# Expert choice for four images at a time, with new stage borders and a new order in one shared PSUM bank

## The reference

```python
for layer in (0, 1):
    sa, ca, ga, sb, cb, gb = (silu(c[layer]) @ wmod[layer]).reshape(32, 6, 1, 128)   # ga, gb: bounded below
    h = layernorm(x) * (1 + ca) + sa
    x = x + ga * attention(h)         # 16 heads of 8; layer 0 with a bias by distance, layer 1 with its own norm
    h = layernorm(x) * (1 + cb) + sb
    logits = h @ gate                 # 8 experts
    # layer 0: the best two experts of each token, with normalised weights; layer 1: the best one
    x = x + gb * sum(weight[e] * expert[e](h) for e in chosen(logits))   # 128 -> 512 -> 128
```

## Time and profile before

| | us |
|---|---|
| median of 3 runs | 2106.24 (2105.88 to 2109.68) |
| profiled execution | 2108.88 |
| its span, first to last instruction | 2107.1 |
| granted TensorE clock, mean | 0.923 |
| PE busy | 1613.4 (77%) |
| DVE busy | 1494.7 (71%) |
| ACT busy | 1137.7 (54%) |
| POOL busy | 667.5 (32%) |

### The profile page before, as it was taken

One profiled execution on the slowest core, in us unless ns is written; L12 is line 12 of the kernel. 1 busy time (PEld: TensorE's weight loads), 2 busy tenths in 40 slices (PEclk: granted clock), 3 DMA queues, 4 the chain that ended last, 5 costly groups with the idle time before them and its releaser, 6 DMA issues. The chain is left out here.

```text
span 2107.1 us, 43953 instructions
## 1 busy us (share of the span) xinstructions
PE 1613.4 (77%) x14050; PEld 1155.9 (55%) x14050; DVE 1494.7 (71%) x4845; ACT 1137.7 (54%) x2198; POOL 667.5 (32%) x740
## 2 busy tenths in 40 slices
PE   2488888888888845999963777877877877843996
PEld 1266565656566624999951444444544444523886
DVE  4478888888888734777744787788888788833664
ACT  0277777777677631222211676666666666641543
POOL 0011323232323252555531223233333333230544
PEclk9899999999999977999985898899999999976998
DMA  3333343333333313222235445455455545415443
GB/s 106 85 69 69 79 79 77 79 76 80 77 79 79 67 39 83 72 72 74 72 104 126 85 95 122 97 108 119 102 108 113 109 101 110 91 59 169 133 125 81
DMA packets 267612, 193.24 MB, mean 92 GB/s; under 512 B 26111, under 2 KB 257441, under 8 KB 266612
## 3 DMA queue, kind: packets, MB, share of 16 engines
q1 hardware_dynamic: 252024, 155.41, 35.2%
q0 software_dynamic: 15360, 35.03, 5.4%
HBM read 95.34 MB, written 53.18 MB: 70 GB/s over the span
## 5 line engine op out<-in xcount | busy, mean ns | idle before, releaser
L923 DVE TENSOR_REDUCE mx<-A 128x2 f32<-128x512 f32 x1024 | 688.4, 682 | 213.7 <-PE A L1173 197.3
L753 ACT ACTIVATE probs<-B 128x1024 f32<-128x1024 f32 x512 | 521.8, 1019 | 281.1 <-PE B L1200 154.6
L1173 PE MATMUL A<-stack 126*128 126x256 bf16 x2048 | 398.3, 284 | 113.4 <-DVE mx L923 92.3
L1200 PE MATMUL B<-stack 128*128 128x256 bf16 x2048 | 367.0, 282 | 67.4 <-DMA stack<-mrow 66.7
L1173 PEld LDWEIGHTS A<-stack 126*128 126x128 bf16 x2048 | 169.6, 100 | 266.8 <-DVE mx L923 165.4
L1218 PE MATMUL M<-probs,vals 128*32 128x256 f32 x4096 | 295.1, 408 | 23.8 <-DVE On L946 19.7
L1200 PEld LDWEIGHTS B<-stack 128*128 128x128 bf16 x2048 | 199.4, 102 | 122.3 <-DMA stack<-mrow 82.0
L640 POOL DMA_INDIRECT gathered<-h,slot_in x192 | 186.9, 974 | 128.6 <-DVE slot_in L1056 82.3
L1629 PE MATMUL A<-w2s,hid 128*128 128x128 f32 x1792 | 219.5, 276 | 8.5 <-issue 8.5
L604 POOL TENSOR_TENSOR parts<-rem,parts 128x512 bf16<-128x512 f32 x64 | 74.5, 1165 | 468.1 <-ACT parts L732 468.1
L1629 PEld LDWEIGHTS A<-w2s,hid 128*128 128x128 f32 x1792 | 208.8, 192 | 12.9 <-issue 11.8
(11 more groups left out here) (182 smaller groups left out, 2405.5 us busy)
## 6 DMA issues: line engine op xcount, KB each, us to landing
stack<-parts SPq DMA_DIRECT2D x768, 64.0 KB
xt<-gathered SPq DMA_DIRECT2D x112, 132.0 KB, 2.2
probs<-gathered SPq DMA_DIRECT2D x40, 256.0 KB
w<-in_w SPq DMA_DIRECT2D x4, 2048.0 KB, 10.1
back_rows<-mod_rows SPq DMA_DIRECT2D x64, 128.0 KB, 3.7
x_mid<-X SPq DMA_DIRECT2D x64, 128.0 KB, 2.9
hid<-expert_out SPq DMA_DIRECT2D x64, 128.0 KB
X<-in_x SPq DMA_DIRECT2D x32, 128.0 KB, 3.8
```

The lines of the kernel that those rows point to most:

```text
L753: act.activation(probs[c % 4][:, :, :, :], Bp[BUFFER[c]][:, :, :, :], ACT.Exp, scale=EXP_SCALE[l][c // 4]).then_inc(b_exp.handle, 1)
L923: dve.tensor_reduce(mx[u][:, h, :], A[h % 2][:, :, :], AX.X, ALU.max).then_inc(a_max.handle, 1)
L1173: ins = pe.matmul(A[h % 2][:, t, :], stack[u][0:n, h, 0, t * P:(t + 1) * P], stack[u][0:n, h, 1, :], start=True, stop=True)
L1200: ins = pe.matmul(Bp[BUFFER[c]][:, j, t, :], stack[u][:, h, 1, t * P:(t + 1) * P], stack[u][:, h, 0, :], start=True, stop=(l == 1))
```

## The change

- GROUP goes from 2 to 4, HELD from 4 to 8, LAG from 5 to 7; an image is scattered at i - 7. The sizes of routing operations double, their number halves. `h3` and the experts' tiles (`w1s`, `w2s`, `hid`) share one piece of SBUF, and `Y` lies in `yt`.
- Setup: the three loads of the modulation go first and have a semaphore of their own; both layers' products are made in separate banks and rows; POOL clears `stack`.
- The experts' weights are loaded in 16 (layer 1: 18) pieces, one at the end of a tick. The padding and the table of tiles are done at the end of attention.
- In layer 1 `load_front` goes from the end of SP's tick to its head and waits for `h_stats` instead of `h_rows`.
- The order of M0's uses: half 1 of the maxima behind chunk 0, then `turn_h2`; `project_v` ahead of chunk 3; half 0 behind product 10 (layer 1) or 12 (layer 0); `count` behind chunk 6. ACT's order follows: half 1 is copied behind exponential 0, `vals` ahead of exponential 3, half 0 behind exponential 5. `place` goes behind the maximum 14.

The core of the diff; moved code that is the same at its new place stands once:

```diff
-GROUP = 2
+GROUP = 4
-HELD = 4
+HELD = 8
+OUT = 4
-LEAD, LAG = 3, 5
+LEAD, LAG = 3, 7
...
-        h3 = sb("h3", [P, HELD, NT, WX])
+        shared = sb("shared", [P, HELD * NT * WX])
+        h3 = shared[:, :].rearrange("p (v t w) -> p v t w", v=HELD, t=NT)
...
+        first_loads = [(cT[:, :, :], a["cT"]), (wmod[:, 0, :], a["wmod0"]), (wmod[:, 1, :], a["wmod1"])]
+        mods = [mod_sb[:, :], hid[0][0:B, 0:3, :].rearrange("b c s -> b (c s)")]
+        mod_cols = [M0[:, 0:6 * B], M1[:, 0:6 * B]]
...
+                for dst, src in first_loads:
+                    sp.dma_start(dst, src).then_inc(first_loaded, 16)
...
-                    sp.dma_start(mod_rows[l], mod_sb[:, :]).then_inc(mod_out, 16)
-                    sp.wait_ge(mod_out, 16 * (l + 1))
+                    sp.dma_start(mod_rows[l], mods[l]).then_inc(mod_out, 16)
...
-                act.wait_ge(loaded, 16 * len(loads))
+                act.wait_ge(first_loaded, 16 * len(first_loads))
...
-                    if l:
-                        pe.wait_ge(moded, 8)
...
+            @block.gpsimd
+            def _(pool):
+                for u in range(2):
+                    pool.memset(stack[u][:, :, :, :], 0.0).then_inc(stack_zero, 1)
...
-                for u in range(2):
-                    dve.memset(stack[u][:, :, :, :], 0.0).then_inc(stack_zero, 1)
...
 def group_done(at, off):
-    return at(off) and at(off)[2] == GROUP - 1
+    return at(off) and at(off)[0] % GROUP == GROUP - 1
...
-            weights = [(w1[:, :, :], a[f"w1_{l}"]), (w2[:, :, :, :], a[f"w2_{l}"])]
+            weights = [piece for e in range(E) for piece in
+                       ((w1[:, e, :], a[f"w1_{l}"][:, e, :]), (w2[:, e, :, :], a[f"w2_{l}"][:, e, :, :]))]
...
             def tick(at):
+                if l and at(3):
+                    load_front(*at(3))
...
-                if l and at(3):
-                    load_front(*at(3))
                 if at(0):
                     stack_max(*at(0), 0)
-            for dst, src in weights:
-                sp.dma_start(dst, src).then_inc(weights_in, 16)
+                if at(-2):
+                    for dst, src in itertools.islice(more_weights, 1):
+                        sp.dma_start(dst, src).then_inc(weights_in, 16)
             run_ticks(tick)
+            sp.dma_start(gathered[l][E * REGION:E * REGION + TAIL * TOK, :].rearrange("(j r) w -> j r w", r=TOK),
+                         pads[E:PADS]).then_inc(padded, 16)
+            sp.wait_ge(run_ready, 1)
+            for e in range(E):
+                r = sp.value_load(run_i[0:1, e:e + 1], min_val=e * REGION, max_val=(e + 1) * REGION - TOK)
+                sp.dma_start(gathered[l][bass.ds(r, TOK), :], pads[e]).then_inc(padded, 16)
+            sp.wait_ge(padded, 16 * (E + 1))
...
-                if at(-5):
-                    scatter(*held(at, -5))
+                if at(-7):
+                    scatter(*held(at, -7))
...
                 chunk(0)
+                step(max_rows, -1, 1)
                 step(head_sums, -2, 1)
...
-                step(max_rows, -1, 1)
                 step(mid_part, 1)
+                step(values, 0)
                 chunk(3)
-                step(values, 0)
...
                 chunk(5)
+                step(max_rows, 0, 0)
...
-                step(max_rows, 0, 0)
                 chunk(7)
...
+                maxima(14, 1)
                 group(l, place, -4)
-                maxima(14, 1)
...
                 a_pass(0, 1)
                 chunk(0)
+                if at(-1):
+                    m0_read((h_ready, 1), (mT_read, -1, 1))
+                    if not at(1):
+                        counted_before()
+                    turn_max(*at(-1), 1)
                 a_pass(2)
                 heads_step(weigh, -2, 3)
                 if at(-3):
-                    m0_read((h_ready, 1), (mT_read, -1, 1), (mT_read, -2, 2))
+                    m0_read((mT_read, -1, 2), (logits_read, -4))
...
                     turn_h2(*held(at, -3))
...
                 a_pass(6)
-                if at(-1):
-                    m0_read((logits_read, -3), (h_ready, 1), (mT_read, -1, 1))
-                    turn_max(*at(-1), 1)
                 heads_step(weigh, -1, 0)
                 a_pass(7)
+                if at(0):
+                    m0_read((logits_read, -3), (mT_read, -1, 2), (h_ready, 1))
+                    project_v(*at(0))
                 chunk(3)
-                if at(0):
-                    m0_read((mT_read, -1, 2), (h_ready, 1))
-                    project_v(*at(0))
...
                 a_pass(10)
+                if l:
+                    turn_first_max()
...
                 heads_step(turn_heads, -1, 0)
-                if group_done(at, -4):
-                    m0_read(*[(x1_ready, -2)] * (l == 0), (base_ready if l else v_ready, 0), (logits_read, -3))
-                    count(*at(-4))
+                if l == 0:
+                    turn_first_max()
                 a_pass(13)
                 chunk(6)
+                if group_done(at, -4):
+                    m0_read((mT_read, 0, 1), *[(x1_ready, -2)] * (l == 0), (logits_read, -3))
+                    count(*at(-4))
...
                 a_pass(15)
-                if at(0):
-                    if group_done(at, -4):
-                        pe.wait_ge(pos_read.handle, pos_read.after(at(-4)[1]))
-                    else:
-                        m0_read(*[(x1_ready, -2)] * (l == 0), (base_ready if l else v_ready, 0))
-                    turn_max(*at(0), 0)
                 chunk(7)
```

More of the change, by code:

```diff
@@ L1 @@
+import itertools
 from contextlib import ExitStack
@@ L247, in build @@
         row_weight = [sb(f"row_weight{u}", [P, 2, NT]) for u in range(2)]
-        row_dest = [sb(f"row_dest{v}", [P, NT], I32) for v in range(HELD)]
-        w1s = [sb(f"w1s{u}", [P, F]) for u in range(2)]
-        w2s = [sb(f"w2s{u}", [P, FC, D]) for u in range(2)]
+        row_dest = [sb(f"row_dest{v}", [P, NT], I32) for v in range(OUT)]
+        w1s = [shared[:, u * F:u * F + F] for u in range(2)]
+        w2s = [shared[:, (2 + u) * F:(3 + u) * F].rearrange("p (c d) -> p c d", c=FC) for u in range(2)]
         row_end = [sb(f"row_end{u}", [P, NT, W - D]) for u in range(2)]
@@ L253, in build @@
         xtT = [sb(f"xtT{u}", [P, TOK]) for u in range(2)]
-        hid = [sb(f"hid{u}", [P, FC, TOK]) for u in range(2)]
-        yt = [sb(f"yt{v}", [P, NT, D]) for v in range(HELD)]
-        Y = [hid[0][:, 2 * u:2 * u + 2, :].rearrange("p c (t d) -> p c t d", t=NT) for u in range(2)]
+        hid = [shared[:, 4 * F + u * FC * TOK:4 * F + (u + 1) * FC * TOK].rearrange("p (c s) -> p c s", c=FC) for u in range(2)]
+        yt = sb("yt", [P, OUT, NT, D])
+        Y = [yt[:, 2 * u:2 * u + 2, :, :] for u in range(2)]
         A = [ctx.enter_context(nc.psum_tensor(f"A{n}", [P, NT, S], F32)) for n in range(2)]
@@ L426, in attention @@
         "gb_row ones_col Y expert_out XR a w1 w2 b1 b2".split())
+    tile_iota, run_i, cnt_i, n_tiles, tile_base, reached, tile_tab, tile_e, tile_row, tile_rev = (g[n] for n in
+        "tile_iota run_i cnt_i n_tiles tile_base reached tile_tab tile_e tile_row tile_rev".split())
+    slots = SLOTS[l]
     n_choice = CHOICES[l]
@@ L778, in weights @@
             def weights(b, k, u):
-                act.wait_ge(w_den.handle, w_den.after(k))
+                act.wait_ge(w_den.handle, w_den.after(b // GROUP))
                 if l:
@@ L1030, in weigh_choices @@
                 row = group_rows(v)
-                dve.wait_ge(w_exp.handle, w_exp.after(k))
+                dve.wait_ge(w_exp.handle, w_exp.after(b // GROUP))
                 if l:
@@ L1042, in place @@
             def place(b, k, u, q, v):
-                dve.wait_ge(pos.handle, pos.after(k))
+                dve.wait_ge(pos.handle, pos.after(b // GROUP))
                 ch.settle()
@@ L1278, in tick @@
                 if at(-3):
-                    m0_read((h_ready, 1), (mT_read, -1, 1), (mT_read, -2, 2))
-                    if not at(-1) and group_done(at, -5):
-                        pe.wait_ge(pos_read.handle, pos_read.after(at(-5)[1]))
+                    m0_read((mT_read, -1, 2), (logits_read, -4))
+                    if not at(-1):
+                        counted_before()
                     turn_h2(*held(at, -3))
@@ L1357, in signals @@
         return [Signal(sem(n), 1) for n in names]
[L1359 to L1360 removed]
     xt_in = Transfers([sem(f"xt_in{u}") for u in range(2)], 1)
[L1362 removed]
+    yt_out = Transfers([sem(f"yt_out{v}") for v in range(OUT)], NT, 0)
     extra_in = Transfers([sem(f"extra_in{u}") for u in range(2)], 1)
@@ L1438, in _ @@
                     scatter(*tile(k, n))
-            for s in range(slots - HELD, slots):
-                pool.wait_ge(yt_out[s % HELD], yt_out.of(s // HELD))
+            for s in range(slots - OUT, slots):
+                pool.wait_ge(yt_out[s % OUT], yt_out.of(s // OUT))
         @block.vector
```

164 lines of the change are left out of this document (80 added, 84 removed).

## The result

The changed kernel takes 1954.93 us (median; 1952.49 to 1960.96) against 2106.49 (2105.88 to 2109.68) for the kernel before on the same chip: a ratio of 0.9282, 95% interval 0.9258 to 0.9306, or some 152 us less. The profiled execution took 1953.77 us, span 1951.8.

The account below looks back on a forecast made before the run. PE was taken as nearly the bound in layer 0's ticks, DVE as busiest in layer 1's long ticks. Savings of 62 + 40 + 13.5 + 8.5 + 3.4 + 10.8 + 15.9 = 154 us gave 1952 us; 8-in-10 range 1900 to 2030.

Parts of the forecast that it names:

- Layer 0's order: New order of M0's uses in layer 0: three quarters of the 41.6 us waits for `mrow` and `vals` go, 31 us.
- First loads: Start of layer 0: `X`, issued behind 4 MB of weights, lands in its usual 3.8 us instead of 12.3: -8.5 us.
- The price of the memset: Setup: each `stack` memset, moved to POOL, takes 7 us, between 3.47 and 18.6, and delays nothing.
- Four ticks ... will take 25.0 + 3 x 20.2: Layer 1, groups of 4: one long tick in four, 85.6 us instead of 90.4, so 4.8 us less.
- The groups' term of -38: Layer 1's ticks: choosing half as often saves 4.8 us per four ticks, in 8 groups 38 us.
- rival C: Layer 1's alternating ticks come from double buffers, not groups; 38 us are missed, 1990 us; chance 0.07.
- the term for fewer choices: Layer 0's ticks: half as many choices give back some 9 of the 25.6 us of waits for `mx`.
- Layer 0's -3.4: Attention 0 to experts 0: table and padding moved ahead -13.5, eight more scatters +10.1; net -3.4 us, between 0 and -5.
- Layer 1's -15.9: Attention 1 to experts 1: 20.9 us go, four more scatters cost 5.0; -10 if the padding lands after the scatters.
- Rival B: Setup: POOL's memsets of 18.6 us each block DVE; 22 us more, 1974 us; chance 0.10.
- A: Rival: borders gain, ticks hardly, since PE's M0 waits only stood before waits for `mx`, which grow; 2016 us; chance 0.18.
- D: Rival: PE stops before `turn_h2` 1.4 us in each of 64 ticks and its clock falls; slower, 2131 us; chance 0.04.

Follow-up runs that it names:

- the weights' experiment: The changed kernel with the experts' weights loaded whole ahead of the ticks again, instead of in 256 KB pieces in the ticks: 1981.84 us (0.9399).

## Why the prediction was right, and where it was not

**Right, by their own steps.** Layer 0's order: three quarters of the 41.6 us of waits, 31; it is 29.8 to 32.9. First loads -8.5: the weights' experiment gives 11.3, a third more. Start of layer 1 -10.8: measured -11.2, 12.4 by the experiment. The signs of the profile were as said: no wait for `vals` or for layer 0's `mrow`, one long tick in four, 24 scatters in a row (708.28 to 738.86 us), `X` read 2.2 us after its issue (said: 4). The price of the memset, 7 us taken between 3.47 and 18.6, is 6.9, and that was luck in part: of the two reasons given, the second doesn't come out (by POOL's row, 1165 ns for 512 columns, 4096 words are 9.3 us, and 7 is three quarters of that), and the first is DVE's rate, taken over for POOL.

**Layer 1, -62 predicted and -63.1 measured, by terms that were wrong.** "Four ticks ... will take 25.0 + 3 x 20.2" is the step that failed, by the assumption that stands behind it, that ticks with no choice are at least as short as those with `count` and `place`. They are not: in the changed kernel the tick with `place` takes 19.6 us and the two with neither 20.4 and 20.1, which takes 1.3 of the 4.8 us. Nor were the 4.8 us the price of choices alone: with groups and order undone, but the other edits in, long and short ticks take 23.8 and 20.9 us in the mean, 2.9 apart, and with the new order and groups of 2 they take 22.8 and 19.6, 3.2 apart. The groups' term of -38 was -4.1 (old order) to -14.4 (new order). Instead the order brought -33.5 to -43.8 where -24 stood, some 40 to 50% of it in PE's own busy time, while PE's granted clock rose, which the sum did not price at all; and moving `load_front`, set at nothing, brought -10. By the traces, step by step: -5.2 for what is left of the other edits, the weights in pieces among them, -10.0 for the front's loads, -33.5 for the order, -14.4 for the groups. Under rival C the same 38 us would have been missed; its mechanism was not at work (one tick in four is long), but most of its price was.

**Layer 0, -40 predicted, -31.6 measured.** The missing 9 us are the term for fewer choices (-9, measured -2.2 to -5.3), and with both edits undone the ticks took 3.5 us more than before.

**The ends.** Layer 0's -3.4, "between 0 and -5", became -7.4: the 10.1 us for eight more scatters were right (9.8), the table and padding gave 12.1 of 13.5, and the new order shortened the pipeline's last ticks by 3 to 5 us, which no term had. Layer 1's -15.9 became -16.2 with other parts: the shift of padding and table gave 15.5 (both undone against before; 20.9 predicted, or less, "if the padding ... lands after the scatters", which it does), the groups took back 7.1 instead of 5.0, and the new order, which had no term here, gave 7.6 to 7.8.

**The setup.** -13.5 predicted, -15.6 measured at the last store. Rival B's block was there and cost 1.36 us in the changed kernel (1.54 against 0.18).

**A and D.** Waits for `mx` did not grow and the old order costs over 70 us, which both speak against A. In front of `turn_max` PE waits 3.5 us in all in attention 0 and 3.3 in attention 1, and in front of `turn_h2` once, 5.0 us, in attention 0, so not in every tick, which speaks against D.

So the total came out by luck: the groups' overprice and the order's and the loads' underprice cancelled. A version with groups of 2 would have been predicted 32 us slower than this one, and it is as fast.

## What to carry to other kernels

Where long and short steps alternate in a pipeline, don't price the cause at their difference: work can pass from the short one to the long one, and the cut between them moves with it. Take the sum of a period, or undo the cause. When an in-order engine waits for a late piece, look at what is queued behind it, as POOL's wait for the front's loads here, even if the engine itself is far from the bound. An edit that makes groups larger in the middle of a pipeline has its price at the end, where the last group is served in a row.

## What the runs showed of the hardware

VectorE's scaling of `silu`, where it meets a memset on GpSimd, waits, and not always equally long: it (0.18 us alone) took 1.4 to 2.0 us in ten profiled executions with both memsets on GpSimd, where it got in when the first one ended, and 8.0 and 8.4 us in two, where it waited for the second as well, though this one starts as the first ends. That is 6.8 us of difference between executions of the same instructions; what decides it is not shown. Other VectorE operations did not wait: beside the same memsets, those of `vals` took 0.96 us and the reciprocal of `silu` 0.55, as in the kernel before. To hold the second memset back until `silu` is scaled might avoid the long wait; it was not tried. The Trainium skill (SBUF — State Buffer, Who interferes with whom) has the rule that, where VectorE works in a two-port mode, whoever issues first holds the port pair that the two share for the whole instruction, and the other waits. The ten rows agree; the two others go further, since there the wait outlasted the instruction that held the pair.

GpSimd's memset runs over 8192 bf16 columns in 6.9 us, while VectorE's is shown as 4096 uint32 in 3.47 us: the packing of zero memsets that the Trainium skill (VectorE: DVE Perf Modes, Zero memsets can be issued as uint32) states for VectorE did not come with the move.
